# Attention: SyncE sends the low parts too, LN2's deviation gets its own key on GpSimd, and the last batch's output tiles are begun while its last unit is weighed

## What is computed

```
x = x + xattn(layernorm(x), ctx, ctx)
x = x + ffn(layernorm(x))

xattn: Q = ln(x) Wq^T + bq,  K = ctx Wk^T + bk,  V = ctx Wv^T + bv
       attn = softmax(Q K^T / sqrt(32)) per head;  out = (attn V) Wo^T + bo
ffn:   logits = h router^T + b;  scores = softmax(logits);  top 2 of 8 experts
       act = (clip(up) + 1) * gate * sigmoid(1.702 gate);  out = sum of scores * (act W_down + b_down)
```

## Time and profile before

| | us |
|---|---|
| median of 3 runs (1800.39 to 1803.59) | 1801.42 |
| the profiled execution, its own time | 1800.36 |
| span of its instructions | 1798.7 |
| PE busy | 1635.6 (91%) |
| DVE busy | 1251.2 (70%) |
| POOL busy | 919.5 (51%) |
| ACT busy | 651.0 (36%) |

### The profile page before, as it was taken

The page is one execution under the profiler, slowest core; times in us unless marked ns, Lnnn a source line. Parts: engine busy times, 40 slices in busy tenths (PEclk is TensorE's granted clock), DMA queues, the critical chain, the costliest instruction groups (busy, mean ns, idle before and its releaser), DMA issues. The chain is left out here.

```text
span 1798.7 us, 30009 instructions
## 1 busy us (share of the span) xinstructions
PE 1635.6 (91%) x9637; PEld 1178.0 (65%) x9637; DVE 1251.2 (70%) x2223; ACT 651.0 (36%) x1265; POOL 919.5 (51%) x859
## 2 busy tenths in 40 slices
PE   4899999999899999999988529999999999999996
PEld 3555555555455555555543229999999998999995
DVE  3676676766666767667655687777888778867874
ACT  3254443534344435344434114223333224322321
POOL 2567767676667675767667211433333333343422
PEclk8999999999999999999999759999999999999998
DMA  5342342423333323333321241324443335333322
GB/s 187 96 126 73 97 115 68 125 83 91 110 85 99 107 77 103 104 83 101 83 77 36 67 170 55 96 82 147 159 148 132 105 130 179 95 101 130 125 71 76
DMA packets 94964, 188.69 MB, mean 105 GB/s; under 512 B 26320, under 2 KB 27344, under 8 KB 94800
## 3 DMA queue, kind: packets, MB, share of 16 engines
q1 hardware_dynamic: 67888, 108.24, 20.2%
q0 software_dynamic: 26912, 78.47, 14.4%
HBM read 204.19 MB, written 37.36 MB: 134 GB/s over the span
## 5 line engine op out<-in xcount | busy, mean ns | idle before, releaser
L657 DVE TENSOR_REDUCE negmax<-max_ps 128x2 f32<-128x1024 f32 x256 | 312.3, 1220 | 230.5 <-PE max_ps L429 229.7
L547 ACT ACTIVATE pt<-work 128x512 f32<-128x512 f32 x512 | 277.7, 595 | 314.1 <-PE work L441 228.8
L1268 PE MATMUL gu_ps<-xgT_hi,wg_hi 128*128 128x256 f32 x1248 | 355.7, 285 | 0.0
L1268 PE MATMUL gu_ps<-xgT_hi,wg_lo 128*128 128x256 f32 x1248 | 352.4, 282 | 0.0
L1268 PE MATMUL gu_ps<-xgT_lo,wg_hi 128*128 128x256 f32 x1248 | 352.1, 282 | 0.0
L743 POOL TENSOR_TENSOR acc<-acc,pt 128x1024 f32<-128x1024 f32 x128 | 301.2, 2367 | 8.2 <-ACT pt L547 7.9
L1507 POOL DMA_INDIRECT out<-acc,idx x78 | 77.3, 991 | 322.5 <-DVE acc L1416 322.5
L1268 PEld LDWEIGHTS gu_ps<-xgT_lo,wg_hi 128*128 128x128 f32 x1248 | 236.1, 189 | 0.0
L1268 PEld LDWEIGHTS gu_ps<-xgT_hi,wg_hi 128*128 128x128 f32 x1248 | 236.0, 189 | 0.0
L1268 PEld LDWEIGHTS gu_ps<-xgT_hi,wg_lo 128*128 128x128 f32 x1248 | 235.9, 189 | 0.0
L429 PE MATMUL max_ps<-ks,qs 96*128 96x512 f32 x512 | 199.9, 472 | 22.4 <-DMA qs<-q_hi 11.0
(11 more groups left out here) (194 smaller groups left out, 2980.8 us busy)
## 6 DMA issues: line engine op xcount, KB each, us to landing
raw_g<-w_gate_up SPq DMA_DIRECT2D x39, 2048.0 KB
raw_d<-w_down SPq DMA_DIRECT2D x39, 1024.0 KB
ks<-k_hi SPq DMA_DIRECT2D x256, 64.0 KB, 2.1
qs<-q_hi SPq DMA_DIRECT2D x256, 64.0 KB, 2.0
bd<-b_down SPq DMA_DIRECT2D x39, 256.0 KB
x_in<-x SPq DMA_DIRECT2D x32, 256.0 KB, 3.1
ctxT_raw<-ctx_t SPq DMA_DIRECT2D x32, 256.0 KB, 4.1
ks<-k_lo POOLq DMA_DIRECT2D x128, 64.0 KB, 2.3
```

The costliest lines, as they stand in the source:

```text
L547: e.activation(pt[k % 2][:, h, :], in_work("exp", u, k, h)[:, :], ACT.Exp, scale=scale).then_inc(exped.sem, 1)
L657: e.tensor_reduce(negmax[:, u % 2, n:n + 2], max_ps[:, :, :], AX.X, ALU.max, negate=True).then_inc(maxed.sem, 1)
L1268: ins = e.matmul(gu_ps[n % GU_BANKS][:, part, :], wg[s][pw][:, k, cols], xgT[s][px][:, k, :], start=(k == 0 and m == 0), stop=(k == KD - 1 ...
```

## The change

Four things are changed.

- **Low parts.** POOL no longer starts the DMAs of the low parts; SP does (`stack_lo` is now under SP, at the key `low`, which stands between SP's high parts). Only unit 0 is shared out otherwise: there SP sends the first of the two high parts of K and of Q, and POOL the second one and the low ones, with semaphores of their own (`first_stacked`).
- **LN2.** The deviation has its own key `rstd`, one round after `x2`, so that POOL takes it after an add and not before it. `ln2` goes from round 2 to round 3 and `turn_xln` from round 4 to round 5 in steps with `c` other than 2 (with `c` = 2 they stay in rounds 4 and 5).
- **Residual.** The load of the residual goes from round 6 to round 7, behind the output projection's second half.
- **Last batch.** An output tile of the last batch is split three chunks to one. The three chunks of the first two tiles go to the end of the last unit's step, into the two banks of `max_ps`; those of the other two go behind the last weighing, ahead of the sum of the weights.

```diff
@@ step(s) @@
             if s - 5 in tokens[:-T]:
                 at(0, ("x2", s - 5))
-                at(4 if c == 2 else 2, ("ln2", s - 5))
-                at(5 if c == 2 else 4, ("turn_xln", s - 5))
+                at(1, ("rstd", s - 5))
+                at(4 if c == 2 else 3, ("ln2", s - 5))
+                at(5, ("turn_xln", s - 5))
                 at(6, ("logits", s - 5))
...
             if s - 1 in tokens:
-                at(6, ("residual", s - 1))
+                at(7, ("residual", s - 1))
...
+            if s == units[-1]:
+                at(7, ("out", tokens[-T], 0), ("out", tokens[-T] + 1, 0))
+            if s == units[-1] + 1:
+                at(1, ("out", tokens[-T] + 2, 0), ("out", tokens[-T] + 3, 0))
             for t in range(T):
                 n = tokens[-T] + t
-                for r, *keys in ((3, ("norm", units[-1], t), ("out", n, 0), ("out", n, 1)), (4, ("x2", n)),
+                for r, *keys in ((3, ("norm", units[-1], t), ("out", n, 1)), (4, ("x2", n), ("rstd", n)),
@@ project_out @@
-                for k in range(half * C // 2, (half + 1) * C // 2):
+                middle = C - 1 if n in tokens[-T:] else C // 2
+                for k in range(middle, C) if half else range(middle):
@@ on_pool @@
-                if kind == "low":
-                    stack_lo(*what)
+                if kind in "kq" and what == [0, 1]:
+                    e.wait_ge(hi_made[kind].sem, hi_made[kind][0])
+                    stack(e, kind, 0, HIGH_AT[kind][1], hi[kind], first_stacked[kind])
+                elif kind == "low" and what[0] == 0:
+                    n = what[1]
+                    e.wait_ge(lo_made[n].sem, lo_made[n][0])
+                    stack(e, n, 0, LOW_AT[n], lo[n], first_stacked[n])
...
-                elif kind == "x2":
+                elif kind == "rstd":
                     ln2_rstd(*what)
@@ on_sp @@
+            def stack_lo(n, u):
+                e.wait_ge(lo_made[n].sem, lo_made[n][u])
+                if u >= RING:
+                    e.wait_ge(exp_ready.sem, exp_ready[u - RING, T - 1, GROUP - 1])
+                stack(e, n, u, LOW_AT[n], lo[n], stacked_lo[n].sem)
...
                 if kind in "kq" and what[1] == 1:
                     stack_hi(kind, what[0])
+                elif kind == "low" and what[0]:
+                    stack_lo(what[1], what[0])
@@ stack, used by both @@
+        def stack(e, n, u, part, source, landed):
+            for r in range(GROUP):
+                e.dma_start((qs if n == "q" else ks)[u % RING][HD * part:HD * (part + 1), r, :].bitcast(F32),
+                            source[HD * r:HD * (r + 1), :].bitcast(F32)).then_inc(landed, 16)
```

More of the change, by code:

```diff
@@ L256, in attention_stage @@
         xln_stored = [Mark(sem(f"xln_stored{t}"), bs, 16) for t in range(T)]
[L257 to L260, removed]
+        HIGH_AT, LOW_AT = {"k": (0, 2), "q": (0, 1)}, {"k": 1, "q": 2}
+        stacked, stacked_lo, first_stacked = {}, {}, {}
+        for n in "kq":
+            stacked[n] = Mark(sem(f"{n}_stacked"), [(0, 0), *[(u, i) for u in units[1:] for i in range(2)]], 16 * GROUP)
+            stacked_lo[n] = Mark(sem(f"{n}_stacked_lo"), units[1:], 16 * GROUP)
+            first_stacked[n] = sem(f"{n}_first_stacked")
+        FIRST = 16 * 2 * GROUP
         m_sent = Mark(sem("m_sent"), units, 32)
@@ L323, in attention_stage @@
                 over = copied, what[0]
-            elif kind == "out" and what[1] == 0:
+            elif kind == "out" and what[1] == 0 and what[0] not in tokens[-T:-T + 2]:
                 over, end = (x2_made, what[0]), ("x2", what[0])
@@ L339, in attention_stage @@
         idle = {("turn_x", 0, t): bank for t, bank in enumerate((max_ps[:, 0, :], max_ps[:, 1, :], o_ps[0][:, :], o_ps[1][:, :]))}
+        idle.update({("out", tokens[-T] + j, 0): max_ps[:, j, :] for j in range(2)})
         in_work = lambda *key: idle[key] if key in idle else work[ring.bank[key]][:, :]
@@ L422, in row_max @@
                 if r == 0:
[L423 to L426, removed]
+                    for n in "kq":
+                        e.wait_ge(stacked[n].sem, stacked[n][u, 1 if u else 0])
+                        if u:
+                            e.wait_ge(stacked_lo[n].sem, stacked_lo[n][u])
+                        else:
+                            e.wait_ge(first_stacked[n], FIRST)
                 for j in range(2):
@@ L779, in stack_hi @@
                     e.wait_ge(exp_ready.sem, exp_ready[u - RING, T - 1, GROUP - 1])
-                dst, places, landed = (qs, (0, 1), q_stacked) if n == "q" else (ks, (0, 2), k_stacked)
-                for part in places:
-                    for r in range(GROUP):
-                        e.dma_start(dst[u % RING][HD * part:HD * (part + 1), r, :].bitcast(F32),
-                                    hi[n][HD * r:HD * (r + 1), :].bitcast(F32)).then_inc(landed.sem, 16)
+                for part in HIGH_AT[n][:2 if u else 1]:
+                    stack(e, n, u, part, hi[n], stacked[n].sem)
+            def stack_lo(n, u):
[3 more added lines that the diff above has]
+                stack(e, n, u, LOW_AT[n], lo[n], stacked_lo[n].sem)
             def send_max(u):
```

20 lines of the change are left out of this document (7 added, 13 removed).

## The result

The changed kernel takes 1778.9 us, the median of four runs (1776.8 to 1780.6). The kernel before took 1801.6 us in the runs on the same chip (1800.4 to 1803.6). The ratio is 0.9872, with a 95% interval of 0.9855 to 0.9889. The profiled execution took 1776.8 us with a span of 1775.1, which is 23.6 us less than before. The forecast was 1781.

The account below looks back on a forecast made before the run. PE bounds the attention stage, so only its idle time and its work at the two ends count: 1800.36 - 28.2 - 6.6 + 2 + 5.3 + 7.1 = 1780.0 us, as a median 1781 us, range 1769 to 1793.

Parts of the forecast that it names:

- Part 1: Attention stage: with the low parts off POOL, PE's waits for ACT before output projection and V go, -28.2 us (0 to -29.9).
- The two long stops: Waits of 4.15 us before the output projection and 4.04 us before V, in steps where POOL idled another 3 to 6 us.
- DVE's share: Row maxima in steps with c = 2: PE's six 1.19 us waits for DVE's late copies go, -6.6 us (0 to -8.7).
- Part 2: SP carries eight more issues a unit: +2 us in middle steps with c = 2, +5.3 us in the first units.
- SP late everywhere: Rival, batches 2 to 7: slow SP issues make each of some 24 steps wait 2 us, 1827 us; chance 0.08.
- +5.3 us: First units: SP's issues in a row delay first maxima, +3.1 us in unit 1 and +2.2 in the third step (0 to +9).
- the start costs nothing: Rival, first steps: PE's projections and DVE's maxima bind there, so SP's issues add nothing, 1776 us; chance 0.08.
- Part 3: LN2's later deviation, scaling and turn, and the residual's later load, cost nothing in the middle.
- Part 4: Last batch: early output tiles put 11 us of matmuls ahead of the sum of the weights, +7.1 us (-2 to +9).
- half the gain: Rival: ACT or DVE stands right behind POOL, so PE gets only half of 34.8 us, 1798 us; chance 0.12.
- early tiles hidden: Rival, last batch: the early matmuls fill time PE would have waited, making that term about -2 us, 1772 us; chance 0.12.
- the slower rival: The rival with SP late in every step, 1827 us; argued against because the slow issues ran beside POOL's own; chance 0.08.

## Why the prediction was right

**Part 1, POOL's blocking: right, and the largest term a little small.** Moving the low parts alone gives 25.8 us net by the medians. The long stretch lost 40.7 us, not 32.8, and two pieces explain more than half of that. The two long stops gave 12.8 us with the ordinary gains of their steps; I had counted 9.4 for them, from the idle rows (4.15 + 4.04 + 1.19). PE's slow matmuls behind a stop stand in no idle row: after the second one four matmuls of the output projection took 3.68 us where 1.98 is usual. Of the waits for K's low part in steps with c = 2 (+2 us) one came, of 0.7 us. The remaining 3 us I cannot assign. Steps with c = 1 gained nothing (30.96 us, forecast 30.7); those with c = 0 and 2 gained 0.2 us more than forecast. Also, POOL's adds are not back to back as I wrote; that costs nothing, since PE releases ACT.

DVE's share (-6.6 us) is confirmed: 7.2 us by the times, and without the new keys the row maxima wait 10.5 us for DVE, not 3.9, which is 6.6. I had taken -6.6 on the grounds that the deviation no longer holds the add up, and that is what the rows of the run without the new keys show. By the Trainium skill (SBUF — State Buffer, section "SBUF: two separate sides") a VectorE operation with two SBUF inputs and a GpSimd operation that reads SBUF keep each other out; the copies at 4.04 us beside an add and 2.34 beside the bias add alone agree.

**Part 2, SP: right in kind, the early term too small.** In the middle the addition was right. SP in the step with c = 2 whose transposed maxima start at 571.59, and PE at its end:

```profile
586.03 2.41 SPq L725 DMA_DIRECT2D qs<-q_lo  x4
...
589.66 6.20 SPq L725 DMA_DIRECT2D ks<-k_hi  x8
...
596.59 2.42 SPq L725 DMA_DIRECT2D ks<-k_lo  x4
...
600.66 0.70 PE L443 MATMUL max_ps<-ks,qs 96*128 96x512 f32 x2 [0.67 <-issue]
```

Q's low part starts 14.4 us into the step (14.3 forecast), and K's last issue begins some 26.8 us into it, against 25.3, because K's eight issues took 6.2 us. The last issue begins at 598.4, and 2.2 us to landing, the median of these four, make 600.6. The maxima start at 600.66 after 0.67 us of idle time for which the profile names no releaser; it is the only step between the maxima of units 4 and 31 in which the first maximum waits so. So "SP late everywhere" did not happen, but in a step with slow issues there was no slack left.

At the start the term that failed is the size of the +5.3 us; the trace says +8.7. Unit 1 came at 60.75, where I had 61.7. Unit 4's first maximum starts 6.75 us later than in the kernel before, where I had 5.3. It inherits 3.1 us (the turned maxima of unit 3 are that much late), as forecast, and adds 3.65 where I had 2.2: I had left K's high part at its old time, but Q's low part now stands ahead of it as well, and it starts at 130.48 us, not 126.28. Then 2.0 us are lost between this maximum and the turned maxima, which I had not counted: after a wait of 4.28 us a pair of matmuls takes 1.19 us, not 0.69. The times give the low parts of units 1 to 4 on SP a price of 11.2 us, the trace 11.8. That is more than 8.7, because with them on POOL unit 0's shared issues stay, and the turned maxima of unit 4 come 3.1 us earlier than in the kernel before. The exact size is loose. Kernels that differ only in their last batch, and the changed kernel itself, had the maxima of unit 4 between 165.1 and 171.8 us in their profiled executions. The three kernels with the low parts of these units on POOL had them at 156.3, 159.4 and 159.7.

By the Trainium skill (DMA: Bandwidth & Descriptors, section "Issuing engines are not separate DMA queues") starting DMAs on a second engine saves only the time that it takes to start them, usually small. Here that is 11.2 us at the start, so the measurement decides against taking it as nothing; the rival "the start costs nothing" is out.

**Part 3: right.** The residual's place is worth nothing, 0.6 us under the changed kernel and inside the noise.

**Part 4, the tail: right in total, composed otherwise.** The stretch grew by 7.7 us (7.1 forecast); the run without it says 8.6. The sum starts 6.4 us later behind the maxima of unit 31 (31.4, not 25.0 us), where I had 8.0, since the last unit's last two scores were pushed back by 4.15 us and not by 5.5; the first residual add 4.4 us later (6.0 forecast), the last 7.2 (7.1). The two errors cancelled: I had the tiles 4.18 us apart, as before, and they are 5.0, since a chunk takes 2.08 and not 1.12 us. The granted clock is 0.50 from 975 to 997 us. That this term came out at 7.1 is in part luck. "Nothing is won after that" was too kind: leaving PE with one chunk a tile loses something.

The rivals: "half the gain" and "early tiles hidden" are out by the runs that undo each part.

**The total is nearer than its parts.** In the profiled execution the middle gave 7.9 us more than forecast, the start cost 3.4 more, the tail 0.6 and what lies behind it 0.7. These errors have opposite signs, and 3.2 us of them are left (1776.8 against 1780.0). The mechanisms held; that the sum fits within 2 us by the medians owes something to luck.

## What to carry to other kernels

Work that another engine is waiting for should never stand on a queue behind a wait for a third engine. Moving the issues and their wait to an engine that does no computing gave the whole gain here. In the short steps at the start its run of issues was too long for the step, so share them out there and not in the middle. Do not pull independent work ahead of the link that starts the last chain: leave it behind that link, where it fills the gaps. That took 10.5 us from the last stretch, making the chain's own members early 4.3, both 14.0. Where a change is worth a few microseconds, read it from its stretch: the same code before it differed by over 6 us from one profiled execution to another.

## What the runs showed of the hardware

- Idle time in the tail came with slower matmuls. With PE busy for 59% of a stretch of 22 us the mean clock was 0.61, with 96% it was 1.00; a chunk of two records took 2.08 us and 1.02 us in them.
- POOL stops for 5.9 to 9.2 us ahead of some of its own DMA issues in the two kernels in which it sends the low parts of all 32 units. In the row of the kernel before the idle time is put down to "issue", and nothing in the trace released it:

```profile
476.56 2.04 POOL L726 DMA_DIRECT2D qs<-q_lo  x4 [9.22 <-issue]
```

  There were two of these in the kernel before and one in the run with the low parts back on POOL, at other places. None is in the traces of the kernels in which SP sends all or most of them. What POOL does in that time stays open.
- SP's eight issues of a high part take 4.95 us as a rule and 5.9 to 6.2 at six places of the changed kernel (five of K, one of Q), where POOL issues nothing. So the slow ones are not due to POOL's issues, as I had argued against the slower rival.
